# Second attention: rows of maxima in one transfer from ScalarE's queue, loads of later groups ahead of the second shares

## What is computed

```python
qkv = (x @ w_qkv).reshape(B, T, 3, H, hd)                  # B, T, H, hd = 4, 1024, 8, 32
scores = jnp.einsum('bhqd,bhkd->bhqk', q, k) * scale
scores = jnp.where(causal[None, None], scores, -jnp.inf)
scores = scores + head_scales[None, :, None, None] * geo    # geo: a rank-one term, folded into q and k by the kernel
attn = jax.nn.softmax(scores, axis=-1)
out = jnp.einsum('bhqk,bhkd->bqhd', attn, v).reshape(B, T, C) @ w_out
```

## Time and profile before

| | |
|---|---|
| median of 3 runs | 1913.09 us (1911.92 to 1913.39) |
| the profiled execution's own time | 1909.37 us |
| its span | 1907.4 us |
| mean granted TensorE clock | 0.961 of full speed |
| TensorE busy | 1795.9 us, 94% |
| VectorE busy | 1429.7 us, 75% |
| ScalarE busy | 1117.3 us, 59% |
| GpSimd busy | 528.6 us, 28% |
| groups of the second attention | from 1148.8 us to about 1535 us of the span |

### The profile page before, as it was taken

One profiled execution on the slowest core, in us unless ns is written; L12 is line 12 of the kernel. 1 busy time (PEld: TensorE's weight loads), 2 busy tenths in 40 slices (PEclk: granted clock), 3 DMA queues, 4 the chain that ended last, 5 costly groups with the idle time before them and its releaser, 6 DMA issues. The chain is left out here.

```text
span 1907.4 us, 34604 instructions
## 1 busy us (share of the span) xinstructions
PE 1795.9 (94%) x12690; PEld 1170.9 (61%) x12690; DVE 1429.7 (75%) x2814; ACT 1117.3 (59%) x2212; POOL 528.6 (28%) x686
## 2 busy tenths in 40 slices
PE   8989999999999999799999989999999987999994
PEld 4545444444444444388888865555555566999994
DVE  7879999999999999367677655466666554766665
ACT  4645888888888888622333214446463632655555
POOL 5760000233000001032223212212525243444444
PEclk9986999999999999899999988999999998999997
DMA  4883744565434502023444255546666334655555
GB/s 170 280 260 53 124 79 96 131 144 122 86 57 73 83 28 85 20 76 111 153 143 147 89 188 120 137 100 156 153 154 156 97 107 147 150 144 144 145 115 196
DMA packets 146600, 239.18 MB, mean 125 GB/s; under 512 B 25830, under 2 KB 81159, under 8 KB 146449
## 3 DMA queue, kind: packets, MB, share of 16 engines
q1 hardware_dynamic: 113312, 171.48, 36.8%
q0 software_dynamic: 17024, 34.25, 7.0%
q10 hardware_dynamic: 16112, 31.46, 4.5%
HBM read 137.49 MB, written 96.60 MB: 123 GB/s over the span
## 5 line engine op out<-in xcount | busy, mean ns | idle before, releaser
L994 DVE TENSOR_REDUCE b_mx<-b_PM 128x1 f32<-128x512 f32 x1024 | 621.0, 679 | 17.9 <-PE b_PM L848 17.5
L970 ACT ACTIVATE b_probs<-b_PS 128x512 f32<-128x512 f32 x1000 | 523.9, 606 | 69.1 <-PE b_PS L902 53.8
L848 PE MATMUL b_PM<-b_kst,b_qst 48*128 48x512 f32 x888 | 280.9, 430 | 0.0
L2919 ACT ACTIVATE d_probs<-d_PS 128x512 f32<-128x512 f32 (+3 forms) x384 | 166.5, 496 | 183.2 <-PE d_PS L2822 182.5
L902 PE MATMUL b_PS<-b_qst,b_kst 50*128 50x512 f32 x744 | 256.9, 436 | 2.1 <-issue 0.2
L2958 DVE TENSOR_REDUCE d_mx<-d_PM 128x2 f32<-128x1024 f32 (+1 forms) x192 | 179.9, 950 | 101.5 <-PE d_PM L2774 59.3
L902 PEld LDWEIGHTS b_PS<-b_qst,b_kst 50*128 50x128 f32 x744 | 120.4, 184 | 163.4 <-ACT b_probs L970 147.4
L2874 POOL TENSOR_SCALAR_AFFINE_SELECT d_probs<-d_probs 128x128 f32<-128x128 f32 x256 | 74.6, 305 | 268.1 <-ACT d_probs L2919 263.4
L790 POOL CAST b_mhalves<-b_maxima 128x16 fp32r<-128x16 f32 x32 | 6.3, 197 | 505.3 <-DVE b_maxima L1003 505.3
L848 PEld LDWEIGHTS b_PM<-b_kst,b_qst 48*128 48x128 f32 x888 | 142.0, 184 | 5.4
L874 PE MATMUL b_PO<-b_probs,x_v 128*32 128x384 f32 (+2 forms) x2048 | 145.2, 390 | 0.0
(11 more groups left out here) (318 smaller groups left out, 3753.9 us busy)
## 6 DMA issues: line engine op xcount, KB each, us to landing
halves<-a_parts SPq DMA_DIRECT2D x7, 2048.0 KB, 8.7
qk<-c_halves ACTq DMA_DIRECT2D x7, 2048.0 KB
w_w<-L_ffn_fc1T SPq DMA_DIRECT2D x12, 1024.0 KB, 5.0
w_w<-L_ffn_fc2T SPq DMA_DIRECT2D x12, 1024.0 KB, 6.3
b_qst<-halves SPq DMA_DIRECT2D x72, 128.0 KB, 4.4
b_kst<-halves SPq DMA_DIRECT2D x72, 128.0 KB, 7.6
d_qst<-qk SPq DMA_DIRECT2D x36, 256.0 KB, 5.2
d_kst<-qk SPq DMA_DIRECT2D x36, 256.0 KB, 7.4
```

The source lines that it names most:

```text
L848: mm = pe.matmul(PM[n % MBANKS][:], qst[buf][at, p, first:first + P], kst[buf][at, p, kh * BLK:(kh + 1) * BLK], start=True, stop=True)
L970: act.activation(probs[:, s % RING], score_bank(g, s)[:], ACT.Exp).then_inc(exped, 1)
L994: dve.tensor_reduce(mx[:, half, (r * PAIRS0 + p) * TPH + t, kh:kh + 1], PM[n % MBANKS][:], AX.X, ALU.max)\
L2919: act.activation(probs[:, s % RING, 0:w], PS[bank(s)][:, 0:w], ACT.Exp).then_inc(exped, 1)
```

## The change

The row transfer becomes one, from all 32 partitions of mrows to both rows of qst, and is issued by ScalarE, for group 0 right after its copy of the rows and later right after the exponential of unit TURN_PLACE (16, the first of round 8). The semaphore rows_in counts 16 for a group instead of 32. On SP's queue rows(g) is gone, and load(g+3) moves from behind load_shares(g-1, 1) to right behind load_shares(g-1, 0), ahead of store_shares(g-1, 1) and sums(g, 0). The condition for the load, that the values of group g-1 are done (pv_done), stays.

```diff
--- before.py
+++ after.py
@@ -2611,7 +2611,7 @@
     GAP = SBANKS
     TURN_PLACE = (TURN + 1) * G1
     LAPS = UNITS + GAP
-    ROW_DMAS = 16 * HALVES1
+    ROW_DMAS = 16
     Q_TURNS = K1_TURNS
     LATE_TOTALS = (10, 6)
     assert STEPS % MTILES == 0 and LAPS % SBANKS == 0 and UNITS % RING == 0 and ROUNDS % PAIRED == 0
@@ -2704,37 +2704,28 @@
                 load_keys1(sp, d, g, qst[hg], kst[hg], q_in[hg])
                 load_values1(sp, d, g, vst[hg], v_in[hg])
 
-            def rows(g):
-
-                sp.wait_ge(m_copied, g + 1)
-                for i in range(HALVES1):
-                    sp.dma_start(qst[g % BUFS][K + i:K + i + 1].bitcast(F32), mrows[i * G1 * TPB:(i + 1) * G1 * TPB, :])\
-                      .then_inc(rows_in, 16)
-
             def sums(g, half):
                 sp.wait_ge(out_copied, g * HPS + half + 2)
                 route.send_sums(sp, outT, g, half)
 
             sp.wait_ge(shared.ffn_stored, shared.FFN_DMAS)
             load(1)
-            rows(0)
             load(2)
             route.load_weights(sp, d)
             for g in range(GROUPS):
                 if g > 0:
                     sums(g - 1, 1)
                     route.load_shares(sp, d, g - 1, 0)
+                if g + BUFS - 1 < GROUPS:
+                    if g > 0:
+
+                        sp.wait_ge(pv_done, g * ROUNDS + RING // G1)
+                    load(g + BUFS - 1)
+                if g > 0:
                     route.store_shares(sp, d, g - 1, 1)
                 sums(g, 0)
-                if g + 1 < GROUPS:
-                    rows(g + 1)
                 if g > 0:
                     route.load_shares(sp, d, g - 1, 1)
-                if g + BUFS - 1 < GROUPS:
-                    if g > 0:
-
-                        sp.wait_ge(pv_done, g * ROUNDS + RING // G1)
-                    load(g + BUFS - 1)
                 if g == GROUPS - 3:
                     route.wait_sums_free(sp, BATCH - 2)
                     weights.load_up(sp, d, bass.ds(0, 1), 0)
@@ -2902,6 +2893,11 @@
                 act.wait_ge(m_turned, g + 1)
                 act.activation(mrows[:], PT[0:HALVES1 * G1 * TPB], ACT.Copy).then_inc(m_copied, 1)
 
+            def rows(g):
+
+                act.wait_ge(m_copied, g + 1)
+                act.dma_start(qst[g % BUFS][K:KM].rearrange("i j n -> i (j n)").bitcast(F32), mrows[:]).then_inc(rows_in, 16)
+
             def copy_out(g, half):
 
                 act.wait_ge(pv_done, g * ROUNDS + HALF_ROUNDS[half] + RING // G1)
@@ -2921,8 +2917,11 @@
 
                     act.wait_ge(rows_in, (g + 1) * ROW_DMAS)
                     copy_rows(g + 1)
+                if s == TURN_PLACE and groups_left(g):
+                    rows(g + 1)
 
             copy_rows(0)
+            rows(0)
             for T in range(TICKS):
                 if T < GROUPS * ROUNDS:
                     g, i = T // ROUNDS, T % ROUNDS
```

More of the change, by code:

```diff
@@ L2726, in _ @@
                     route.load_shares(sp, d, g - 1, 0)
-                    route.store_shares(sp, d, g - 1, 1)
-                sums(g, 0)
-                if g + 1 < GROUPS:
-                    rows(g + 1)
-                if g > 0:
-                    route.load_shares(sp, d, g - 1, 1)
                 if g + BUFS - 1 < GROUPS:
@@ L2737, in _ @@
                     load(g + BUFS - 1)
+                if g > 0:
+                    route.store_shares(sp, d, g - 1, 1)
+                sums(g, 0)
+                if g > 0:
+                    route.load_shares(sp, d, g - 1, 1)
                 if g == GROUPS - 3:
```

## The result

The changed kernel takes 1962.48 us (1951.8 to 1964.76, 5 runs) against 1913.39 us for the kernel before, measured beside it. The ratio is 1.0231, with a 95% interval from 1.0206 to 1.0256: slower by 2.3%, some 44 to 49 us. The forecast was 1923.5 us, range 1899 to 1934. The sign was right; the size was not, and the time lies outside the range.

The account below looks back on a forecast made before the run. TensorE, 94% busy and waiting 8.1 us for late kst loads, was taken as the bound. -13.7 + 5.5 (totals) + 10.6 (shares) + 5.6 + 2.3 (clock) = +10.3 us gave 1923.5 us, range 1899 to 1934.

Parts of the forecast that it names:

- Rows from ScalarE ... 0: ScalarE's row issues, 16 in all, fit its idle time after rounds 8 and 9: 0, upper end 6 us.
- the clock term: TensorE's low clock after stands: -5.6 us for ended waits, +5.6 for three long new stands, +2.3 for five short.
- What bounds the kernel: TensorE, busy 94%, waits 8.1 us for kst loads in round 6; ending this and its low clock gains 13.7 us.
- A small transfer behind a load lands with the load's end: On SP's in-order queue, totals come 15.1 us after the load's first issue; the shares' load can issue after 14.7 us.
- Totals, 5.5 us in five short groups: Late totals of half 0 hold VectorE 2.8 us, TensorE 1.1 us, in groups 1, 2, 3, 7 and 11.
- Shares of half 1, 10.6 us: Late shares hold VectorE, and TensorE with it, 2.4 us in group 4 and 4.1 us each in groups 8, 12.
- At the start ... 0: Loads 2 and 3 and the weights go out earlier at the start; TensorE waits for none there: 0.
- rival E: Rows on two engines land late at round 0, 1.45 us in each of five short groups; 1906.7 us, chance 0.06.
- ScalarE's issue at 0: Each row issue takes ScalarE 0.37 us, covered by 2.05 us of idle time after rounds 8 and 9: 0.
- Rival A: Only the waits for loads go, totals land sooner and VectorE's slack absorbs the rest; 1899.4 us, chance 0.28.
- Rival D: SP's queue becomes a chain, each load later than the last, all eight stands growing; about 1935 us, chance 0.09.

Follow-up runs that it names:

- e9: Kernel before with only the load moved, rows still issued by SP as two transfers; 1952.23 us, ratio 1.0197.
- e4: Kernel before with the load of the shares split into two transfers, one for each head; 1901.51 us, ratio 0.993.
- e11: The kernel of e4 unchanged, measured again in more rounds against the kernel before; 1897.13 us, ratio 0.9914.
- e3: Changed kernel, load still moved, with the rows as two transfers from ScalarE; 1952.34 us, ratio 1.0201.
- e10: e6 with SP again holding load 2, the weights and load 3 until the first rows are copied; 1904.27 us, ratio 0.9959.
- e1: Changed kernel with the load back in its old place, rows as one transfer from ScalarE; 1928.59 us, ratio 1.0066.
- e6: Changed kernel with the load of the shares split into two transfers, one for each head; 1917.45 us, ratio 1.0016.
- e2: Kernel before with the rows issued by ScalarE as two transfers, load in its old place; 1919.96 us, ratio 1.003.

## Why the prediction was wrong

The step that failed is "Rows from ScalarE ... 0", and with it the clock term. TensorE stood 24.5 us for the rows, and the lower clock added 21.8 us of busy time where a net 2.3 us was counted. The terms in turn:

- **What bounds the kernel: right.** No wait for kst is left in the changed kernel. Its gain of 13.7 us was never seen by itself, since e9, the moved load alone, is slower; but e4 and e11, which end these waits in another way, gain 13 and 16 us.
- **A small transfer behind a load lands with the load's end: right**, in queue order and in figures where GpSimd moved nothing. The shares of half 1 in group 4 went on 1271.10 - 1256.61 = 14.5 us after the load (14.7 forecast); the totals in group 1 took 16.2 us (15.1 forecast).
- **Totals, 5.5 us in five short groups: hidden here.** VectorE waited longer than the 2.8 us forecast, 3.1 to 7.5 us in these groups, as the lag of group 2 in the old trace was applied to groups where GpSimd's transfers start with the moved load. But TensorE had already stood for the rows, and no wait for the take of round 1 is seen after it. Where e3 shortens the row waits, those waits are 7.2 us, near the forecast. The longer groups were put at 0; TensorE stood 1.1 us in each of groups 7 and 11 for the totals behind the loads of groups 6 and 10.
- **Shares of half 1, 10.6 us, the largest term: too large.** VectorE waited 2.6 us in group 4 (2.4 forecast), 1.2 in group 8 and 0 in group 12 (4.1 each). The shares were late as forecast, but VectorE, itself held up by then, came later too. TensorE stood 1.7 us for it, in one place.
- **"At the start ... 0": wrong.** Loads 2 and 3 were found harmless because TensorE waits for none of them. But the rows of group 0 have to pass them: 5.2 us of stand, gone in e10. Asked was who waits for the moved transfers, not who shares the engines with them.
- **The rows, put at 0 in the sum, rival E at 0.06: the step that failed.** The mechanism, two engines that also end a load, was named, with 1.45 us in each of five groups; it came to eight stands of up to 5.2 us, 24.5 us. Three runs show it. Two transfers in place of one bring 24.5 down to 8.0 us (e3), the old place of the load brings it to 16.5 (e1), and the shares' load split, with rows and loads as they are, to 6.5 (e6). The Trainium skill, "DMA: Bandwidth & Descriptors", section "Why a DMA increments its semaphore by 16 and not by 1", lets the slowest dimensions of both sides set the number of engines. The traces agree: the DMA share is 0.14 while the load of group 1 ends, and in e6, with the leading dimension of 2 cut from the shares' load, the totals behind this load come 3.6 us sooner.
- **ScalarE's issue at 0: small, not 0.** One issue took 0.63 us. With one, the score product of round 11 waits 0.84 to 0.86 us for ScalarE in groups 5, 9 and 13 of the changed kernel, where it waited 0.64 us before; with two, in e2, it waits 1.5 us.
- **The clock, net +2.3 us: the term most off beside the rows.** It was priced from falls that followed stands of at most 2.8 us, 1.9 us for each of three and a quarter of that for five. The lower level held for 76.3 us in place of 25.0. Falls of 13.7 us came behind stands of 4.6 and 5.0 us, but also behind one of 1.66 us and, in e4 and e6, with none above 0.3 us in the 15 us before; so the stand's length alone does not give the price.

The sign is in part luck. Of the idle time forecast, -8.1 + 5.5 + 10.6 = +8.0 us, the two terms that made it positive came to some 4 us, less than the 8.1 us gained. Without the rows, which the sum had at 0, and the clock the same sum would have said faster. The idle time came out at 17.7 + 5.1 us.

Rival A, no new waits, is refuted by the result and its trace. Rival D, a chain on SP's queue that runs away, is not seen: the load starts 7.3 us into group 2 (1206.45 - 1199.16) and 9.4 us into group 3 (1233.38 - 1223.97), with stands of rounds 0 to 2 in the difference; in group 4 it is at 8.4 us again.

## What to carry to other kernels

Before a large transfer is moved, list every small transfer that will be in flight beside it, on whichever queue, and when each is due; the one that counts may come from another engine's queue. Look at the DMA share of a transfer that runs alone: here a share of 0.13, two engines' worth of sixteen, delayed the end of the 2 MB load behind it. Splitting it by its leading dimension was worth more than any reordering here. Where a change adds stands of TensorE, give the slow clock behind them a wide range: here it cost as much as the stands, about the same for a few of 4 to 5 us (the changed kernel) as for many of 1 to 3 us (e3), and two profiles of one kernel differed by 5.8 us of it.

## What the runs showed of the hardware

- A queue pushes back on its issuer: behind a load, two issues of 2 KB totals took 6.24 to 9.26 us in the five short groups of the changed kernel. With the shares' load split, those of group 1 took 1.16 us.
- Two engines' worth of sixteen decide when a 2 MB load is done: the DMA share is 0.14 while it ends, and with the shares' load split the totals behind the load came 12.6 us after its issue in place of 16.2.
- Issued from ScalarE's queue, rows get past SP's load only in part. As one transfer, issued at 1190.48 in group 1, they let TensorE start at 1199.16, 8.7 us later, when the load that SP had issued from 1183.77 was ending; as two (e3), issued at 1190.17, 7.4 us later. Over the stage the waits are 24.5 and 8.0 us.
- The same edit of the rows changed the kernel's time only from 1952.3 to 1962.5 us, with intervals of the ratio that overlap (1.0161 to 1.024, 1.0206 to 1.0256): the second wait stood right behind the first, and the clock was low for 77.2 and 76.3 us.
- The granted clock can fall to 0.50 for 13 us with TensorE busy for 11.29 of the 12 us before (e6 from 1302.5), and in another execution stay at 1.00 after the same (e10).
